# Fourteen filler products on constants in the second attention of a four-layer kernel

## The reference

```python
k_eff = (W_dq.T @ W_uq.T @ W_uk).reshape(nh, hs, kvl)
c_kv = x @ W_dkv.T
q = (x @ W_dq.T @ W_uq.T).reshape(B, T, nh, hs).transpose(0, 2, 1, 3)
q_lat = jnp.einsum('bhtd,hdl->bhtl', q, k_eff)
attn = jnp.einsum('bhtl,bsl->bhts', q_lat, c_kv) / math.sqrt(hs)
attn = jnp.where(causal_mask[None, None], -jnp.inf, attn)
attn = jax.nn.softmax(attn, axis=-1)
ctx = jnp.einsum('bhts,bsl->bhtl', attn, c_kv)
y = jnp.einsum('bhtl,hld->bhtd', ctx, v_eff).transpose(0, 2, 1, 3).reshape(B, T, C)
```

## Time and profile before

| | us |
|---|---|
| median of 3 timed runs | 2094.85 |
| lowest, highest | 2094.42, 2110.43 |
| the profiled execution, its time | 2097.97 |
| the profiled execution, its span | 2096.2 |
| second attention, first maximum to first slot | 1358.50 to 1397.93 |
| unit 0, from its slot 0 to unit 1's | 1397.93 to 1449.36 |
| unit 2, from its slot 0 to unit 3's | 1489.75 to 1530.14 |

### The profile page before, as it was taken

How to read it: one execution, slowest core, us unless ns; L and a number is a source line. 1 busy time by engine, 2 the same in 40 slices (tenths; PEclk the granted TensorE clock), 3 DMA queues, 4 the chain that set the end, 5 groups by cost and what they waited for, 6 DMA issues and landing times. The chain is left out here.

```text
span 2096.2 us, 32175 instructions
## 1 busy us (share of the span) xinstructions
PE 1784.5 (85%) x10624; PEld 762.0 (36%) x10624; DVE 1485.2 (71%) x1466; ACT 1322.1 (63%) x2671; POOL 898.0 (43%) x574
## 2 busy tenths in 40 slices
PE   7669899899978777777777779989999998999996
PEld 2222222233344444434444424333444434233332
DVE  3667877888469999999999944455666634456446
ACT  4316666577779999989999723334555563554343
POOL 1057787730069999999999930010000001000000
PEclk9758999899988888899888889968999997999998
DMA  2335555530278988978889620402332200000000
GB/s 105 134 115 198 179 200 182 195 99 13 72 251 307 327 298 304 312 279 304 299 305 312 230 81 0 106 31 44 58 54 39 40 2 16 0 1 0 0 5 16
DMA packets 86546, 288.88 MB, mean 138 GB/s; under 512 B 11671, under 2 KB 15026, under 8 KB 84383
## 3 DMA queue, kind: packets, MB, share of 16 engines
q1 hardware_dynamic: 72319, 236.57, 35.5%
q0 software_dynamic: 13824, 50.34, 6.2%
q10 hardware_dynamic: 288, 0.45, 0.1%
HBM read 214.60 MB, written 61.21 MB: 132 GB/s over the span
## 5 line engine op out<-in xcount | busy, mean ns | idle before, releaser
L555 DVE TENSOR_REDUCE attn_mx<-banks 128x1 f32<-128x1024 f32 (+7 forms) x512 | 501.1, 989 | 181.5 <-PE banks L362 102.1
L1637 POOL TENSOR_TENSOR hc<-st,ct 128x1024 f32<-128x1024 f32 x256 | 599.8, 2401 | 9.5 <-DVE st L1596 9.2
L1596 DVE TENSOR_TENSOR_SCAN st<-da,banks 128x1024 f32<-128x1024 f32 x256 | 562.8, 2266 | 18.6 <-ACT da L1553 7.8
L507 ACT ACTIVATE attn_probs<-banks 128x512 f32<-128x512 f32 (+3 forms) x640 | 307.4, 533 | 210.2 <-PE banks L392 106.1
L1561 ACT ACTIVATE ut<-b_turned,mats 128x128 f32<-128x128 f32 x1024 | 311.6, 387 | 1.7
L1553 ACT ACTIVATE da<-dt,mats 128x1024 f32<-128x1024 f32 x256 | 282.8, 1138 | 28.2 <-DVE st L1596 19.7
L392 PE MATMUL banks<-attn_qa,attn_ka 75*128 75x512 bf16 (+3 forms) x896 | 279.6, 381 | 4.2 <-DMA attn_qa<-attn_mrow 1.8
L1478 PE MATMUL banks<-hc,onecol 128*32 128x512 f32 x1024 | 159.9, 701 | 102.3 <-POOL onecol L1635 80.2
L360 PE MATMUL banks<-attn_ka,attn_qa 64*128 64x512 bf16 (+3 forms) x512 | 203.1, 398 | 37.6 <-DVE attn_mx L555 28.9
L731 POOL TENSOR_TENSOR made_ahead<-b_turned,x_turned 128x1024 f32<-128x1024 f32 x96 | 184.1, 1917 | 43.9 <-DMA ahead<-made_ahead 42.2
L1454 PE MATMUL banks<-mats,ut 128*128 128x128 f32 x1024 | 167.2, 305 | 35.3 <-DVE st L1596 21.6
(11 more groups left out here) (437 smaller groups left out, 1982.8 us busy)
## 6 DMA issues: line engine op xcount, KB each, us to landing
dt<-dt_rows SPq DMA_DIRECT2D x256, 512.0 KB, 5.7
ahead<-made_ahead POOLq DMA_DIRECT2D x96, 512.0 KB, 3.1
ua<-ahead SPq DMA_DIRECT2D x96, 512.0 KB, 6.1
attn_qa<-q_lin SPq DMA_DIRECT2D x144, 64.0 KB
attn_qu<-attn_qa SPq DMA_DIRECT2D x16, 512.0 KB, 4.3
attn_ka<-k_lin SPq DMA_DIRECT2D x72, 64.0 KB
moe_w<-in_moe_w SPq DMA_DIRECT2D x2, 2048.0 KB, 10.2
mats<-in_mats SPq DMA_DIRECT2D x1, 2876.5 KB, 12.8
```

What stands on the lines that cost most here:

```text
L507: nc.scalar.activation(probs[s % 4][:, jj, c0:BLK], scores_exp[jj][:, c0:BLK], ACT.Exp, scale=scale).then_inc(probs_ready, 1)
L555: nc.vector.reduce_max(mx[:, qt, j:j + 1], scores_max[n % 2][:, 0:w], AX.X)\
L1596: nc.vector.tensor_tensor_scan(st[n % 4][:, :], da[n % 4][:, :], pair[:, :, :].rearrange("p h t -> p (h t)"), 0.0, ALU.mult, ALU.add).then ...
L1637: nc.gpsimd.tensor_tensor(hc[n % 8][:, :], st[n % 4][:, :], ct[:, b * SEQ:(b + 1) * SEQ], ALU.mult)\
```

## The change

A function `filler` is added to PE's program: one matmul of the bf16 identity (128 rows, 128 columns) by the same identity repeated to 512 columns. It has no reader: the bank it writes is written anew, with its start flag, before anything reads it. It is called in two places, for the causal attention alone. In the opening it comes after each of the maxima 23 to 28, into bank 4. In unit 0 it comes at the start of slots 1, 2, 3, 4 (after a wait for the first copy of turned maxima) and 7, 8, 9, 10 (after a wait for the second), into bank 7.

```diff
+                def filler(bank):
+                    nc.tensor.matmul(bank, ident_b[:, :], ident_b[:, :].unsqueeze(1).to_broadcast([128, 4, 128]),
+                                     start=True, stop=True)
+
                 def body(i):
                     for s in range(NE):
                         odd = s % 2 == 1
+                        if causal and i == 0 and s in (1, 2, 3, 4, 7, 8, 9, 10):
+                            pe.wait_ge(mrow_ready[0 if s < 7 else 1], 1)
+                            filler(turned[:, :])
                         if odd and s > 1:
...
                 for n in range(own_from):
                     max_unit(0, n)
                     front.tensor_second(pe, n)
+                    if causal and n >= own_from - 6:
+                        filler(scores_exp[0][:, :])
```

## The result

The changed kernel takes 2086.15 us, the kernel before 2100.43 us (medians of 16 executions each, taken side by side). The ratio is 0.9937 with a 95% interval of 0.9912 to 0.9963: 13 us less, between 8 and 18. Forecast were 2084 and 10.8 us less. The two overlap around 0.995, which is near the 0.9948 that 2084 over 2094.85 stands for. One of the sixteen executions of the changed kernel, at 3731.56 us, was in a slow state and is left out of the ratio. The other executions of one and the same kernel lie some 30 us apart, so it is the profiles that tell where time went.

The account below looks back on a forecast made before the run. TensorE was taken to set the pace at half clock in unit 0, VectorE in the opening. The terms -9.6 - 2.3 + 1.1 = -10.8 us gave 2084 us against the median 2094.85, range 2080 to 2097.

Parts of the forecast that it names:

- The gain, slots 4 to 13: Unit 0 of the second attention, at the upper clock level, goes at unit 2's pace: 25.52 - 15.89 = 9.6 us saved.
- The gain, slots 0 to 4: Start of unit 0: slot 4 starts 7.7 us behind slot 0 instead of 10.06, 2.3 us saved; bounds 1.4 and 3.2.
- The prices: Opening's six fillers and those of slots 1 to 4 cost nothing; slots 7 to 10 cost 4 x 0.27 = 1.1 us.
- The new wait: Slots 7 to 10: fillers wait for ScalarE's copy of the second half's turned maxima, done well before; costs nothing.
- The reading of the forms ahead of the two rises: Before both clock rises PE ran 128 by 128 products, in the low stretch smaller ones; so full-array fillers keep the clock up.
- That unit 0 holds as units 1 to 7 do: Unit 0 with fillers keeps the upper clock, as the later units, running the same slots, do at 1.00 throughout.
- the rival's sum, -0.3: Clock falls again between slots 3 and 4 of unit 0: -2.3 + 2.0 = -0.3 us, so 2094.5; chance 0.12.
- Everything behind unit 0 moves forward by the same amount: All work after unit 0 starts earlier by what unit 0 saves, so the whole kernel gains 10.8 us.
- warning that the course of the clock differs from execution to execution: At unit 0 the clock's course may vary between executions, so one profile tells little of the median; named as the main risk.
- its range: Whole kernel: 2080 to 2097 us, taking in the forecast, the shorter stretch and the clock's fall between slots 3 and 4.

Follow-up runs that it names:

- the opening's six alone: Changed kernel with the eight fillers of unit 0's slots left out, only the opening's six kept; slot 13 at 32.51 us, first maximum to the end 740.4 us.
- the kernel without 1 to 4: Changed kernel with the fillers of slots 1 to 4 left out, the other ten kept; slot 13 at 23.83 us, first maximum to the end 734.2 us.
- the changed kernel delayed: Changed kernel plus eight more fillers in slots 15 to 22 of unit 1; slot 13 at 34.06 us, first maximum to the end 743.8 us.
- the second (6, from -1 to 14): Second timing of the unedited changed kernel beside the kernel before; ratio 0.9970 (0.9934 to 1.0006).

## Why the prediction was right

*The gain, slots 4 to 13.* 25.52 us became 15.88 without the fillers of slots 7 to 10 (23.57 - 7.69) and 16.72 with them: 9.64, as worked out from unit 2, whenever the clock holds.

*The gain, slots 0 to 4.* 7.68 us, forecast 7.7, but by two errors that cancel. Without fillers in slots 1 to 4 and at the upper level slot 4 starts at 7.11, with the opening's six alone and in the kernel without 1 to 4. With them it starts at 7.68, also in the changed kernel delayed, whose opening is that of the six alone. So the path itself is 0.6 us shorter than the 6.04 + 1.7 read from unit 2, and the four fillers, put at nothing, cost 0.57. The rows are the last wide reduction and the start of slot 4, with the opening's six alone (slot 0 at 1393.55):

```profile
1397.78 1.23 DVE L564 TENSOR_REDUCE attn_mx<-banks 128x1 f32<-128x1024 f32 x1 [0.42 <-PE banks L362]
1400.66 0.27 PE L392 MATMUL banks<-attn_qa,attn_ka 75*128 75x256 bf16 x1
```

and in the changed kernel delayed (slot 0 at 1386.17):

```profile
1390.74 1.22 DVE L567 TENSOR_REDUCE attn_mx<-banks 128x1 f32<-128x1024 f32 x1 [0.76 <-PE banks L362]
1393.86 0.27 PE L392 MATMUL banks<-attn_qa,attn_ka 75*128 75x256 bf16 x1
```

VectorE waits for PE ahead of this reduction, longer with the fillers, and the reduction ends 5.79 us behind slot 0 instead of 5.46; the filler of slot 4 adds the rest. PE's idle 0.96 us come behind the fillers of slots 1 to 3 and cannot cover them, since these delay the very maximum that VectorE, and then PE, waits for.

*The prices.* The opening's fillers cost nothing (39.38 against 39.43; 41.57 against 41.54). Those of slots 7 to 10 cost 0.21 us each, not 0.27, and at the lower level 0.48. The 0.27 was misread: at 1505.07 the second L392 starts 0.22 us after the first, and the rest of the 0.53 lies between it and the L360 behind it. The load of weights was no reason for a higher price, since each filler has a load of its own (PE and PEld both count 10638 in the changed kernel). The 215.7 ns of the Trainium skill, page "TensorE: Matmul & The Clock Gate", section "Wait — 56ns, not 53.3ns?", agrees with the runs to 0.01 us. With these terms slot 13 comes out at -9.64 - 2.95 + 0.57 + 0.83 = -11.2 us, as measured. The new wait cost nothing; its margin was a microsecond, less than reckoned, since the prediction counted to slot 8 and the first filler with that wait stands in slot 7.

*Why the clock stays up.* The reading of the forms ahead of the two rises is borne out in one half. Fillers as long over 64 rows left the clock at 0.50, with PE busy 40.05 of 40.60 us. The Trainium skill, page "TensorE: Matmul & The Clock Gate", section "Part 1: The HAM clock gate", sets the clock by how busy the engine has been; the runs do not agree, if the profile's busy time is meant. The other half, that the 32 columns of L412 were a reason for the low clock, has the profile of the 32-column fillers against it. Both halves rest on one profile each; fillers with other values than the identity's were not tried, and the cause in the clock itself stays open.

*That unit 0 holds as units 1 to 7 do* is the step that carried least. Units 1 to 7 are not at 1.00 throughout, as the prediction has it: in the kernel before the clock falls in unit 7, and so it does in every profile of this case, for 6.8 us or more.

```profile
1705.60:1712.30 6.70, 6.63 (x38) 2.74 (x38) 0.00 (x0) 3.83 (x8) 0.00 (x0) 0.50 0.01 2
```

Nine of the fourteen profiles, the two of the changed kernel among them, also have a fall of 3.4 us in slot 3 of one of the units 2 to 6, and one of these nine has two. The step held in both profiles of the changed kernel, and failed in the third execution of the same code up to there. Of the rival's sum, -0.3, the low price of the fillers was right (1.9 against 2.0); the gain left was 1.9 instead of 0.3, since the clock also rose earlier, 31.9 instead of 35.2 us behind slot 0.

*"Everything behind unit 0 moves forward by the same amount"* failed. Of 11.2 us, 1.4 came back in unit 4 and 3.5 in the end part, through lower clock there. The forecast of 10.8 for the whole was met by the first timing (13, from 8 to 18); the second (6, from -1 to 14) lies lower and does not exclude it, and the profiles from the first maximum on speak for about 6. That the measured 2086 came so near to 2084 is therefore in part luck: about 5.6 us were given back that the sum did not have, and the kernel before took 2100.43 in that timing, not the 2094.85 from which 2084 was reckoned. The prediction's warning that the course of the clock differs from execution to execution was the right one, but it stood there for unit 0 alone, and its range went by the median of three executions of a kernel whose single times spread over 30 us.

## What to carry to other kernels

Where TensorE is busy and its granted clock is at the lower level, compare the stretch with the same code at the upper level elsewhere in the trace: the difference is what the clock costs, and here it came back to 0.1 us. In this kernel products on constants over all 128 rows of the array held or raised the clock at some offsets and not at others. They cost nothing right ahead of a wait, and 0.21 us each where TensorE is the pace. Ahead of the products that another engine waits for they cost too (0.57 us for four), even though TensorE is idle for longer than that a little later. Before the gain is booked, look at every later stretch in which the clock falls: a shift of the work against the clock can take as much as the fillers gave, so more than one profile is needed. Compare two kernels only between profiles in which the clock has the same course up to the change; otherwise a part of the difference is the offset and not the edit.

## What the runs showed of the hardware

PE's busy time in the profile did not tell the two levels of the clock apart here: 23.7 of 23.7 us busy at 0.50 in one kernel, 6.98 of 8.00 busy at 1.00 in another, in the same layer. With fillers of 128 rows by 32 columns unit 0 ran at 1.00, with fillers of 64 rows by 128 columns at 0.50, in one profile each. The opening took one of a few times (39.4, 40.1, 40.3 to 40.5, 41.5 us, and 43.2 once), and in the two pairs of profiles of the same code that share one, all that follows repeats to 0.1 us, though the layers ahead differ by 3.8 us in one pair and 13.2 in the other. What ties the work to these few offsets is not settled.
